# A feed-forward's first-of-equals mask moved from TensorE and ACT to DVE, with relu multiplied by the turned mask straight from PSUM

## The reference

```python
inter = xf @ c1_w.T @ c2_w.T                     # rank 16, 1792 columns
blk = inter.reshape(B * T, 56, 32)
idx = jnp.argmax(blk, axis=-1) + jnp.arange(0, 1792, 32)
h = relu(einsum('bkm,bm->bk', w1[idx], xf))      # one row of w1 per block of 32
out = einsum('bk,bkm->bm', h, w2t[idx])
x = layernorm(x + out)
```

## Time and profile before

| | us |
|---|---|
| median of 3 runs | 894.89 (891.84 to 899.7) |
| the profiled execution | 896.81 |
| its span, first to last instruction | 895.1 |
| TensorE busy | 846.2 (95%) |
| DVE busy | 566.6 (63%) |
| ACT busy | 417.1 (47%) |
| POOL busy | 278.9 (31%) |
| mean granted TensorE clock | 0.971 |

### The profile page before, as it was taken

One profiled execution on the slowest core, in us unless ns is written; L12 is line 12 of the kernel. 1 busy time (PEld: TensorE's weight loads), 2 busy tenths in 40 slices (PEclk: granted clock), 3 DMA queues, 4 the chain that ended last, 5 costly groups with the idle time before them and its releaser, 6 DMA issues. The chain is left out here.

```text
span 895.1 us, 11899 instructions
## 1 busy us (share of the span) xinstructions
PE 846.2 (95%) x4316; PEld 504.7 (56%) x4344; DVE 566.6 (63%) x772; ACT 417.1 (47%) x777; POOL 278.9 (31%) x324
## 2 busy tenths in 40 slices
PE   7999999999999999999986689999999999999995
PEld 5866333333333333333455467777777777777773
DVE  5588889899998999985054774326533564245404
ACT  4321687787788787777711023332222222222221
POOL 2213235633663364114205024333112121122221
PEclk9999799899999999999989799999999999999998
DMA  6793342334543443234153331210400030002001
GB/s 211 252 281 120 88 101 80 99 116 116 149 136 104 128 144 97 83 116 114 46 181 95 141 107 60 83 60 1 131 12 1 0 118 1 1 1 94 1 1 47
DMA packets 48225, 83.07 MB, mean 93 GB/s; under 512 B 9544, under 2 KB 13640, under 8 KB 48040
## 3 DMA queue, kind: packets, MB, share of 16 engines
q1 hardware_dynamic: 40448, 64.45, 23.2%
q0 software_dynamic: 7440, 16.76, 6.2%
q10 hardware_dynamic: 280, 1.11, 0.4%
HBM read 54.18 MB, written 28.05 MB: 92 GB/s over the span
## 5 line engine op out<-in xcount | busy, mean ns | idle before, releaser
L517 DVE TENSOR_REDUCE neg_max<-ps_pair 128x2 f32<-128x1024 f32 x256 | 303.3, 1217 | 31.1 <-PE ps_pair L632 30.7
L483 ACT ACTIVATE probs<-ps_st 128x512 f32<-128x512 f32 x512 | 267.4, 604 | 72.5 <-PE ps_st L645 72.4
L645 PE MATMUL ps_st<-q,k 50*128 50x512 f32 x512 | 158.3, 479 | 0.4 <-ACT probs L483 0.2
L882 POOL TENSOR_TENSOR g_l<-picked,g_h 128x512 fp32r<-128x512 f32 x56 | 73.1, 1306 | 268.0 <-ACT g_h L941 268.0
L645 PEld LDWEIGHTS ps_st<-q,k 50*128 50x128 f32 x512 | 69.8, 188 | 145.5 <-ACT probs L483 141.3
L659 PE MATMUL ps_pv<-probs,v 128*32 128x512 f32 x1024 | 139.5, 617 | 0.0
L927 ACT ACTIVATE mask_t<-ps_t 128x512 bf16<-128x512 bf16 x56 | 33.4, 597 | 186.0 <-PE ps_t L1152 186.0
L632 PE MATMUL ps_pair<-k,q 48*128 48x512 f32 x512 | 106.9, 450 | 8.4 <-DVE neg_max L517 8.1
L999 DVE TENSOR_REDUCE top<-ps_prep 128x14 f32<-128x448 f32 x62 | 38.6, 623 | 98.8 <-PE ps_prep L1128 98.7
L1164 PE MATMUL ps_h<-xt_h,w_h 128*128 128x512 f32 x224 | 93.5, 418 | 0.0
L1164 PE MATMUL ps_h<-xt_h,w_l 128*128 128x512 f32 x224 | 88.9, 397 | 0.0
(11 more groups left out here) (146 smaller groups left out, 1148.3 us busy)
## 6 DMA issues: line engine op xcount, KB each, us to landing
operands<-parts POOLq DMA_DIRECT2D x20, 512.0 KB, 4.1
q<-operands SPq DMA_DIRECT2D x64, 128.0 KB, 2.5
sums<-stage SPq DMA_DIRECT2D x32, 256.0 KB, 2.3
x_raw<-xT SPq DMA_DIRECT2D x16, 256.0 KB, 5.1
k<-operands SPq DMA_DIRECT2D x64, 64.0 KB, 2.4
q<-operands SPq DMA_DIRECT2D x64, 64.0 KB, 2.5
att<-sums SPq DMA_DIRECT2D x16, 256.0 KB
yf<-x SPq DMA_DIRECT2D x4, 1024.0 KB, 5.5
```

Source lines behind the costliest of these rows:

```text
L483: nc.scalar.activation(probs[kt % 2][:, r], ps_st[i % 3][:], ACT.Exp, scale=float(HD) ** -0.5).then_inc(exp_done, 1)
L517: nc.vector.tensor_reduce(neg_max[:, at:at + 2], ps_max[pair % 2][:], AX.X, ALU.max, negate=True).then_inc(max_red, 1)
L645: nc.tensor.matmul(ps_st[i % 3][:], k_[n % QR][64 * a:64 * a + ROWS, kt * P:(kt + 1) * P], q[n % QR][64 * a:64 * a + ROWS, j, :], start=Tr ...
L882: nc.gpsimd.tensor_tensor(g_l[m % 2][:], picked[m % 2][:], g_h[m % 2][:].bitcast(F32), ALU.subtract).then_inc(g_ready, 1)
```

## The change

The first of equal maxima is found by DVE. After the comparison, which now writes to `marked` and not to `mask`, DVE multiplies the marks by descending ranks (32 for a block's first column down to 1 for its last), reduces each block to its largest (`best`), and compares the ranked marks with it into `mask`; each of the three waits for the one before. `first_marks` and ACT's copy `turn` go. `pick` multiplies relu by the turned mask, read straight from PSUM, and there are two banks `ps_t` in place of `ps_t` and `ps_z`. The second front bank is `ps_h` in place of `ps_z`, so the first `inner_up` waits until all front steps have been read out. The ranks are set by 32 memsets on POOL ahead of its first square root.

```diff
+        rank = sb("rank", [P, CH // BLK, BLK], BF16)
+        marked = sb("marked", [P, CH // BLK, BLK], BF16)
+        best = sb("best", [P, CH // BLK], BF16)
...
-        ps_h, ps_z, ps_prep = ps("ps_h", [P, S]), ps("ps_z", [P, S]), ps("ps_prep", [P, S])
-        ps_t = ps("ps_t", [P, S], BF16)
+        ps_h, ps_prep = ps("ps_h", [P, S]), ps("ps_prep", [P, S])
+        ps_t = [ps(f"ps_t{j}", [P, S], BF16) for j in range(2)]
...
-            return (ps_prep, ps_z)[FRONT.index(s) % 2]
+            return (ps_prep, ps_h)[FRONT.index(s) % 2]
...
+            for k in range(BLK):
+                nc.gpsimd.memset(rank[:, :, k], float(BLK - k)).then_inc(ranked, 1)
             pool.wait_ge(half_set, 1)
             root(0)
...
-            turn(0, 0)
...
                     relu(b, m)
-                    if b * MT + m + 1 < NB * MT:
-                        turn(*divmod(b * MT + m + 1, MT))
                     high_g(b, m)
...
-                    nc.vector.tensor_tensor(
-                        mask[:, t, c * CH:(c + 1) * CH].rearrange("p (n k) -> p n k", k=BLK), src,
-                        top[t % 2][:].rearrange("p (n o) -> p n o", o=1).broadcast_to([P, CH // BLK, BLK]),
-                        ALU.is_equal).then_inc(prep_done, 1)
+                    nc.vector.tensor_tensor(marked[:], src, spread(top[t % 2]), ALU.is_equal).then_inc(prep_done, 1)
+                    dve.wait_ge(prep_done, n + 1)
+                    nc.vector.tensor_tensor(marked[:], marked[:], rank[:], ALU.mult).then_inc(weighed, 1)
+                    dve.wait_ge(weighed, i + 1)
+                    nc.vector.tensor_reduce(best[:], marked[:], AX.X, ALU.max).then_inc(bested, 1)
+                    dve.wait_ge(bested, i + 1)
+                    nc.vector.tensor_tensor(mask[:, t, c * CH:(c + 1) * CH].rearrange("p (n k) -> p n k", k=BLK),
+                                            marked[:], spread(best), ALU.is_equal).then_inc(first_marked, 1)
...
-                dve.wait_ge(z_done, i + 1)
+                dve.wait_ge(mask_turned, i + 1)
                 dve.wait_ge(relu_ready, i + 1)
-                nc.vector.scalar_tensor_tensor(picked[m % 2][:], ps_z[:], 1.0, picked[m % 2][:], ALU.is_equal,
-                                               ALU.mult).then_inc(picked_ready, 1)
+                nc.vector.tensor_tensor(picked[m % 2][:], ps_t[m % 2][:], picked[m % 2][:], ALU.mult
+                                        ).then_inc(picked_ready, 1)
...
-                if i:
-                    pe.wait_ge(mask_t_ready, i)
+                if i >= 2:
+                    pe.wait_ge(picked_ready, i - 1)
...
                     if i:
                         pe.wait_ge(relu_ready, i)
+                    else:
+                        pe.wait_ge(prep_done, len(FRONT))
...
-                    first_marks(b, m)
```

More of the change, by code:

```diff
@@ L734, in _feed_forward @@
         mask = sb("mask", [P, TT, INTER], BF16)
-        mask_t = [sb(f"mask_t{j}", [P, S], BF16) for j in range(2)]
+        rank = sb("rank", [P, CH // BLK, BLK], BF16)
+        marked = sb("marked", [P, CH // BLK, BLK], BF16)
+        best = sb("best", [P, CH // BLK], BF16)
         picked = [sb(f"picked{j}", [P, S]) for j in range(2)]
@@ L743, in _feed_forward @@
         ps_out = [pairs[t // 2][:, t % 2] for t in range(TT)]
[L744 to L745 removed]
+        ps_h, ps_prep = ps("ps_h", [P, S]), ps("ps_prep", [P, S])
+        ps_t = [ps(f"ps_t{j}", [P, S], BF16) for j in range(2)]
         x_in = [sem(f"xf_in{j}") for j in range(2)]
         prep_mm, prep_half, prep_done = sem("prep_mm"), sem("prep_half"), sem("prep_done")
[L749 to L751 removed]
+        first_marked = sem("first_marked")
+        mask_turned, ranked, weighed, bested = sem("mask_turned"), sem("ranked"), sem("weighed"), sem("bested")
+        h_done, relu_ready, picked_ready = sem("h_done"), sem("relu_ready"), sem("picked_ready")
         g_high, g_ready, out_mm = sem("g_high"), sem("g_ready"), sem("out_mm")
@@ L785, in number, with number_of_marks @@
             return ORDER.index((b, s))
+        MARKS = [(b, s - TT - 1) for b, s in ORDER if s > U]
+        def number_of_marks(b, c, t):
+            return MARKS.index((b, c * TT + t))
         def front_bank(s):
-            return (ps_prep, ps_z)[FRONT.index(s) % 2]
+            return (ps_prep, ps_h)[FRONT.index(s) % 2]
         @block.sync
@@ L921, in _ @@
         def _(act):
[L922 to L927, removed]
             def relu(b, m):
@@ L1003, in step @@
                         dve.wait_ge(mask_turned, MT * (b - 1) + min(MT, -(-(c + 1) * CH // P)))
-                    nc.vector.tensor_tensor(
-                        mask[:, t, c * CH:(c + 1) * CH].rearrange("p (n k) -> p n k", k=BLK), src,
-                        top[t % 2][:].rearrange("p (n o) -> p n o", o=1).broadcast_to([P, CH // BLK, BLK]),
-                        ALU.is_equal).then_inc(prep_done, 1)
+                    i = number_of_marks(b, c, t)
+                    if i == 0:
+                        dve.wait_ge(ranked, BLK)
+                    spread = lambda tile: tile[:].rearrange("p (n o) -> p n o", o=1).broadcast_to([P, CH // BLK, BLK])
+                    nc.vector.tensor_tensor(marked[:], src, spread(top[t % 2]), ALU.is_equal).then_inc(prep_done, 1)
[6 more added lines that the diff above has]
+                                            marked[:], spread(best), ALU.is_equal).then_inc(first_marked, 1)
             def pick(b, m):
                 i = b * MT + m
-                dve.wait_ge(z_done, i + 1)
+                dve.wait_ge(mask_turned, i + 1)
                 dve.wait_ge(relu_ready, i + 1)
-                nc.vector.scalar_tensor_tensor(picked[m % 2][:], ps_z[:], 1.0, picked[m % 2][:], ALU.is_equal,
-                                               ALU.mult).then_inc(picked_ready, 1)
+                nc.vector.tensor_tensor(picked[m % 2][:], ps_t[m % 2][:], picked[m % 2][:], ALU.mult
+                                        ).then_inc(picked_ready, 1)
             def add_residual(b, t):
@@ L1146, in turn_mask @@
                 i = b * MT + m
-                pe.wait_ge(prep_done, number(b, marks(-(-(m + 1) * P // CH) - 1, TT - 1)) + 1)
-                if i:
-                    pe.wait_ge(mask_t_ready, i)
+                c = -(-(m + 1) * P // CH) - 1
+                pe.wait_ge(first_marked, number_of_marks(b, c, TT - 1) + 1)
+                if i >= 2:
+                    pe.wait_ge(picked_ready, i - 1)
                 for t in range(TT):
-                    last = nc.tensor.transpose(ps_t[:, t * P:(t + 1) * P], mask[:, t, m * P:(m + 1) * P], ident16[:])
+                    last = nc.tensor.transpose(ps_t[m % 2][:, t * P:(t + 1) * P], mask[:, t, m * P:(m + 1) * P], ident16[:])
                 last.then_inc(mask_turned, 1)
@@ L1167, in inner_up @@
                     last.then_inc(h_done, 1)
[L1169 to L1175, removed]
             def inner_down(b, m, ts):
```

## The result

The changed kernel takes 912.9 us (median of 4 runs, 911.36 to 919.96); the kernel before, beside it, 894.85. The ratio is 1.021 [1.0164, 1.0256], so the change makes the kernel slower, by about 2%. The forecast was 914.4 us. The profiled execution took 911.36 us.

A forecast was written before the change was run, and what follows sets the result against it. TensorE was taken to bound the kernel before, with DVE nearly unbroken in slots 0 to 2 of batches 1 to 3. Waits of 32.2 us added less 12.7 saved gave +19.5 on 894.9: 914.4 us, range 901 to 924.

The forecast's parts named there:

- DVE's load is hidden: Rival, chance 0.08: TensorE gets its 12.7 us and at most the front's 7.1 is lost, 882 to 889 us.
- The saving: On TensorE's chain, first_marks goes: 55 x 0.23 = 12.7 us less.
- The mask step: On DVE, a mask step grows from 1.19 to 2.95 us, bounds 1.9 and 3.2.
- Cheap marks: Rival, chance 0.1: the three new DVE instructions come near their floor, a step is 1.9 us, total 890 to 896.
- The added waits: TensorE waiting on DVE in the front and batches 0 to 3: 7.1 + 3.9 + 7.4 + 7.4 + 6.4 = 32.2 us.
- 2.1 + 0.3, 3.6 and 1.4: TensorE's waits in batch 1 for the third, fourth, fifth and sixth marks, the last with small waits: 7.4 us.
- Batch 0: First mark at 519.79, a normalization in place of additions and statistics: added waits 0.9 + 1.9 + 0.3 + 0.8 = 3.9 us.
- The hold: POOL's low_g holds DVE's multiplication 0.76 us in two-step slots (0, 1, 6, 7) and a normalization 0.75.
- the rival had 7.8: Rival "no hold", chance 0.2: POOL does not hold DVE on 2-byte operands, 914.4 - 7.8 = 907 us.
- Batch 3: Slot 2 loses its second step, slot 3's inner_down waits 2.8 us for the late pick; 6.4 us added in all.
- dearer: Rival, chance 0.12: a step of 3.18 us adds 4.1, clock loss 1.6 each in batches 1 and 2; 918 to 922.
- The other costs at nothing: pick stays 0.70 us; 32 rank memsets hide in POOL's 6.75 us idle; turn_mask's wait and two mask banks change nothing.

The follow-up runs named there:

- no_rank: The changed kernel without its three new DVE instructions; the first comparison writes straight into mask: 880.64 us, ratio 0.9837 to the kernel before.
- balanced: The changed kernel with mask steps reordered, one in each of slots 0 to 7 of batches 1 to 3: 894.96 us, ratio 0.9999 to the kernel before.
- no_hold: The changed kernel with POOL's subtraction for g_l replaced by two memsets of the same tile: 907.39 us, ratio 1.0139 to the kernel before.
- early_up: The changed kernel with the first inner_up waiting for eight front steps, not nine: 908.88 to 915.04 us, ratio 1.0165 to the kernel before.
- changed_third: The changed kernel, nothing edited, run for a third profiled execution: 922.37 us.
- front_order: The changed kernel with the last output projection between the front's mask steps and norm(2) between second and third: 904.33 us, ratio 1.0106 to the kernel before.
- changed_again: The changed kernel, nothing edited, run for one more profiled execution: 912.4 us.

## Why the prediction was right, point by point

**The mechanism.** DVE in slots 0 to 2, not TensorE, sets the pace; no_rank takes DVE's load away and balanced moves it, and in both the waits of batches 1 to 3 go. The rival "DVE's load is hidden" falls with the waits at 626.09 and 636.06. That the forecast sum and the feed-forward of the first profile after agree to 0.1 us is luck: by the other two executions of the changed kernel the sum is 18.7 and 22.3, by the medians 18, and terms that were too large and too small offset each other, as follows.

**The saving.** 12.7 was forecast; the four batches of no_rank are 13.3 us shorter than before. In the slots without a wait the step from relu to relu went from 6.25 to 5.97, 0.28 and not 0.23. Of the 0.05, 0.04 is `inner_down`: its 12 matmuls take 2.76 us on the chain before (from 606.53) and 2.72 after (from 676.79), both at a granted clock of 1.00; why isn't shown.

**The mask step.** 2.95 forecast, 2.94 measured. The multiplication is 0.39 long and 0.43 from start to start, which is the term of the sum; second reduction and last comparison are 0.62 each, as taken. "Cheap marks" falls: the new instructions stand 0.43, 0.65 and 0.55 us apart. The Trainium skill (VectorE: DVE Perf Modes, the perf-mode tier table) gives two elements a cycle to a two-tensor operation on bf16 data in SBUF; by that line alone the last comparison would be as short as the multiplication. The Trainium skill (Vector Engine (DVE) Microarchitecture Reference, section 5.1) reports one element a cycle for a two-source operation with 2-byte operands that reads one element 16 times. 448 columns took 0.62 in the comparison, which repeats each element 32 times, and 0.39 in the multiplication, which repeats nothing, so the second page is borne out.

**The added waits**, changed less no_rank by the table, to which the front's 1.5 for its bank is added:

```
            forecast   measured
front          7.1        6.6     (53.5 - 46.9)
batch 0        3.9        4.6
batch 1        7.4        7.1
batch 2        7.4        7.1
batch 3        6.4        7.5
sum           32.2       32.9
```

32.9 less 13.3 is the 19.5 measured, but for rounding; the forecast was 32.2 less 12.7. In batch 1 the terms were 2.1 + 0.3, 3.6 and 1.4; slots 1, 2 and 3 are longer than in no_rank by 2.6, 3.6 and 0.8. TensorE's idle time in the rows is less, 0.46 + 1.26, 3.22 and 0.36: each of these four waits made its slot longer by 0.4 us more than the idle time in front of the row. A list of waits therefore understates the loss, here 5.3 us for 7.0.

Batch 0 was under-sized by 0.7. The walk had no hold there by POOL's other subtraction, for `w_l`; four last comparisons in batch 0 last 0.93 to 0.95 us beside it:

```profile
528.21 1.43 POOL L882 TENSOR_TENSOR w_l<-w_raw,w_h 128x512 fp32r<-128x512 f32 x1
...
529.19 0.93 DVE L1014 TENSOR_TENSOR mask<-marked,best 128x448 bf16<-128x448 bf16 x1
```

Whether that makes up the 0.7 isn't shown.

**The hold** was over-sized, and this the sum hides. (The POOL row at 231.72 that it was taken from, `att<-att,inv`, is a multiplication in the kernel and not a subtraction; both read two SBUF tensors.) "0.76" is 1.05 - 0.39 = 0.66, since it ended 0.24 behind POOL's subtraction (621.13 against 620.89, rows at 620.08 and 619.60) and not a whole 0.39, and all began a little earlier; the normalization's "0.75" is 2.44 - 1.91 = 0.53 (639.58 against the earlier trace rows). Over the kernel no_hold is worth 5.3 us, about 6 at equal clock, where the rival had 7.8.

**Batch 3** was under-sized by 1.1. The wait for `g_l` was forecast at 2.8; the timeline has it at 2.52:

```profile
830.83 1.28 POOL L890 TENSOR_TENSOR g_l<-picked,g_h 128x512 fp32r<-128x512 f32 x1 [3.19 <-ACT g_h L944]
...
832.17 0.50 PE L1192 MATMUL ps_pair<-w_h,g_h 128*128 128x512 f32 x1 [2.52 <-POOL g_l L890]
```

Behind it the granted clock was 0.58 (windows row):

```profile
832.20:835.00 2.80, 2.80 (x8) 2.17 (x9) 2.70 (x6) 0.00 (x0) 0.00 (x0) 0.58 0.43 165
```

0.42 x 2.8 is 1.2 us, about the difference. In early_up's profile there is the same wait, and batch 3 is 1.3 us shorter:

```profile
837.18 0.50 PE L1192 MATMUL ps_pair<-w_h,g_h 128*128 128x512 f32 x1 [2.52 <-POOL g_l L890]
837.52 0.40 PE L1192 MATMUL ps_pair<-w_l,g_h 128*128 128x512 f32 x1
```

The clock stayed at 1.00 behind it (windows row):

```profile
838.00:842.00 4.00, 4.00 (x22) 3.15 (x21) 3.26 (x6) 0.57 (x1) 0.00 (x0) 1.00 0.70 262
```

**The rival "dearer"** was half right: its step price is wrong, but its loss of clock, put at batches 1 and 2, is real in some executions. It was seen in changed_third, early_up and front_order (both batches) and in no_hold (batch 2), not in the first profile nor in changed_again, and makes part of the spread from 911.4 to 922.4 us.

**The other costs at nothing** held: `pick` 0.68 against 0.70; the 32 memsets took 2.08 us, overlapping, and POOL then still waited 4.74 for the first variance, as the row at 456.04 shows.

## What to carry to other kernels

An engine's mean share tells nothing about whether it can take more work; lay out its instructions slot by slot against the engine it feeds, and the places where it falls behind come out, here with a sum that was right in part by luck. Work that was moved to such an engine should be dealt out anew: here the move by itself cost 19.5 us of feed-forward, and the same instructions, one mask step per slot and a projection in the front's idle time, took 8.7 off the kernel before. A change is judged fairly only in an order that was fitted to it, and the kernel before deserves the same (it had 4.5 us lying in its front).

## What was not expected of the hardware

The same wait of TensorE, 3.2 us in the same place, is followed by a granted clock of 1.00 in one execution and 0.50 in the next (0.5 to 1.8 us each time). With the attention's code unchanged, the first square root behind it started anywhere between 454.8 and 464.3 us in the profiled executions (no_rank and changed_third), more than most of the effects studied here, so that small changes were told by a part of the trace and not by the time. POOL's memsets did not hold DVE's two-input multiplication at all (394 ns at most), its subtraction did (1057); but the normalization, which reads one tile and two columns of numbers, was longer beside a memset too (2.23 us against 1.91).
